# Routed rows kept on chip and filed whole into a slot-ordered DRAM buffer, in a cross-attention and mixture-of-experts layer

## The reference

```python
x = x + attention(layernorm(x), ctx)
X = layernorm(x).reshape(16384, 512)
scores = sigmoid(X @ gate_w.T)                      # 32 experts
_, idx = top_k(scores + bias, 4)
w = scores[idx] / sum(scores[idx])
pos = place of this choice among all choices of its expert, in token order
valid = pos < 512
xe[expert, pos] = X[token] where valid              # 32 x 512 x 512
ye = (silu(xe @ W1) * (xe @ W3)) @ W2               # inner width 256
out = sum over the 4 choices of w * ye[expert, pos] (0 where not valid)
out = out + (silu(X @ sw1.T) * (X @ sw3.T)) @ sw2.T
x = x + out
```

## Time and profile before

| | |
|---|---|
| time, median of 3 runs | 1765.65 us |
| lowest and highest | 1764.72 and 1767.5 us |
| the profiled execution's own time | 1765.1 us |
| its span in the trace | 1763.3 us |
| mean granted clock of TensorE, share of full speed | 0.975 |
| PE, DVE, POOL, ACT busy | 93%, 78%, 71%, 60% |
| moved by the DMAs | 293.75 MB, 167 GB/s |

### The profile page before, as it was taken

The page is one execution under the profiler, slowest core; times in us unless marked ns, Lnnn a source line. Parts: engine busy times, 40 slices in busy tenths (PEclk is TensorE's granted clock), DMA queues, the critical chain, the costliest instruction groups (busy, mean ns, idle before and its releaser), DMA issues. The chain is left out here.

```text
span 1763.3 us, 31937 instructions
## 1 busy us (share of the span) xinstructions
PE 1636.3 (93%) x9056; PEld 1020.9 (58%) x9056; DVE 1379.1 (78%) x3486; ACT 1066.7 (60%) x2368; POOL 1253.2 (71%) x1104
## 2 busy tenths in 40 slices
PE   5999999999999999999999999999758999999991
PEld 4566666666666666656666665655335555555550
DVE  5679988887998888889888888999636777677771
ACT  5676776767777677777767777775323444444440
POOL 2327777777777777777777777777776777887864
PEclk8999999999999999999999999999889999999995
DMA  7546776777776666678676667787439789998665
GB/s 255 150 128 162 196 167 165 172 169 158 166 187 174 156 174 165 158 174 189 161 155 174 164 161 181 178 202 164 125 121 280 154 179 166 203 214 153 100 91 74
DMA packets 474532, 293.75 MB, mean 167 GB/s; under 512 B 342643, under 2 KB 385397, under 8 KB 474356
## 3 DMA queue, kind: packets, MB, share of 16 engines
q1 hardware_dynamic: 429300, 239.03, 53.1%
q0 software_dynamic: 45056, 52.67, 18.4%
HBM read 135.06 MB, written 110.17 MB: 139 GB/s over the span
## 5 line engine op out<-in xcount | busy, mean ns | idle before, releaser
L923 POOL DMA_INDIRECT slot_table<-tok_line,slot x480 | 508.3, 1059 | 135.9 <-issue 126.3
L932 POOL TENSOR_TENSOR xt_l<-xt,xt_h 128x512 fp32r<-128x512 f32 x128 | 165.0, 1289 | 159.2 <-ACT xt_h L758 159.2
L799 ACT ACTIVATE prob<-S_ps,rs 128x512 f32<-128x512 f32 x128 | 88.1, 688 | 254.8 <-DVE S_ps L1295 248.3
L485 PE MATMUL S_ps<-a_h,xt_h 128*128 128x512 f32 x512 | 211.5, 413 | 3.4 <-DVE m_l L1268 3.3
L500 PE MATMUL O_ps<-m_h,pt_h 128*128 128x512 f16 x512 | 196.2, 383 | 14.5 <-DMA pt_l<-p_l 12.9
L485 PE MATMUL S_ps<-a_h,xt_l 128*128 128x512 f32 x512 | 200.9, 392 | 0.0
L485 PE MATMUL S_ps<-a_l,xt_h 128*128 128x512 f32 x512 | 200.8, 392 | 0.0
L500 PE MATMUL O_ps<-m_l,pt_h 128*128 128x512 f16 x512 | 194.7, 380 | 0.0
L500 PE MATMUL O_ps<-m_h,pt_l 128*128 128x512 f16 x512 | 194.7, 380 | 0.0
L947 POOL TENSOR_TENSOR prob<-prob,rsum 128x512 f32<-128x512 f32 x128 | 135.6, 1059 | 80.8 <-DVE rsum L1323 74.4
L1567 POOL DMA_INDIRECT out<-ye,idx_far x80 | 125.5, 1569 | 46.3 <-issue 22.7
(11 more groups left out here) (245 smaller groups left out, 4773.3 us busy)
## 6 DMA issues: line engine op xcount, KB each, us to landing
xt<-in_xT SPq DMA_DIRECT2D x128, 256.0 KB
xr<-in_x SPq DMA_DIRECT2D x64, 512.0 KB, 3.8
x2aug<-x SPq DMA_DIRECT2D x128, 256.0 KB
out<-xr SPq DMA_DIRECT2D x64, 512.0 KB, 3.4
up_more<-in_w SPq DMA_DIRECT2D x36, 256.0 KB, 5.0
slot_table<-tok_line,slot POOLq DMA_INDIRECT x512, 2.1
up_w<-in_w SPq DMA_DIRECT2D x28, 256.0 KB, 4.3
down_more<-in_w SPq DMA_DIRECT2D x18, 256.0 KB, 6.2
```

What stands on the lines that cost most here:

```text
L485: last = pe.matmul(S_ps[t % 2][:, :], left[:, kc, :], right[:, b % 2, kc, :], start=(m == 0), stop=(m == 3 * KD - 1))
L799: act.activation(prob[:, t % 2, :, :], S_ps[t % 2][:, :].rearrange("p (h j) -> p h j", h=H), ACT.Exp, scale=rs[:, q % 2, 0, t % 2:t % 2 + ...
L923: pool.indirect_dma_start(table, bass.IndirectOffsetOnAxis(ap=slot[:, g % 2, i, q:q + 1], axis=0), tok_line[:, g % 2, i, :], None, bounds_ ...
L932: pool.tensor_tensor(xt_l[:, t % 2, :, :], xt[:, t % 2, :, :], xt_h[:, t % 2, :, :].bitcast(F32), ALU.subtract).then_inc(xt_lo, 1)
```

## The change

The token's row, its 32 weights and its number are now put side by side in one on-chip row of 560 floats (2,240 bytes). A ring `kept` of nine such tiles takes the place of `x2`, `wfull` and `tok_line`; the last two tiles go into two buffers that are free by then (`aside`). POOL's indirect DMA writes the whole row into a DRAM buffer `slot_rows` at the token's slot. An expert's 512 rows thus lie one behind the other, and SP loads them with one plain DMA (`load_rows`). `x2aug`, `slot_table`, the stores of rows and weights, the loads of slot numbers and the 128 gathers are gone. A scatter-add takes its row numbers from the loaded rows.

Empty slots must hold zero rows, so `slot_rows` is blanked first: 32 stores of 128 x 2,240 floats (1.147 MB), two in each step `n` from 1 to 16 (`fill_slots`). ACT's `rows_scaled(t)` newly waits until tile t-9 has been filed, for tiles 5 to 8 until all blanks are stored. `TABLE` is 21 instead of 20, `wk` and `wv` share one buffer and are loaded anew for each pair of batches (`load_kv`, 14 loads of 768 KB). The ring of expert rows has 5 places instead of 6, that of `ye` 3 instead of 4, and SP loads the rows of expert e when expert e-5 has landed in `out`, with the weights of expert e+5 behind.

In an expert's step PE, ACT and DVE take the turns and the down products in alternation.

The diff, cut to its core:

```diff
-ROW = D + E
+LINE = 16
+ROW = D + E + LINE
+ROWS_KEPT, ASIDE = 9, B * S // P - 2
...
+                def fill_slots(e):
+                    if e == 0:
+                        sp.wait_ge(zero_set, 3)
+                    sp.dma_start(slots_of[e], blank).then_inc(fill_stored, 16)
...
-                    for r in range(TOKENS, TOKENS + PAD, P):
-                        sp.dma_start(x2aug[r:r + P, :], zrow).then_inc(fill_stored, 16)
-                        sp.dma_start(out[r:r + P, :], zrow[:, 0:D]).then_inc(fill_stored, 16)
-                    sp.wait_ge(zero_set, 3)
-                    sp.dma_start(table.rearrange("(e p c) l -> p e (c l)", e=E, p=P),
-                                 fill.rearrange("p (e c) -> p e c", e=E)).then_inc(fill_stored, 16)
+                        sp.dma_start(out[r:r + P, :], zrow).then_inc(pad_stored, 16)
...
+                    for e in range(2 * n - 2, 2 * n):
+                        if 0 <= e < E:
+                            fill_slots(e)
...
                 def rows_scaled(t):
-                    after(act, x2_lo, t - 1)
-                    after(act, x2_stored[t % 2], t // 2 * 16)
-                    act.activation(x2[:, t % 2, :], x_tile(t), ACT.Identity,
+                    if ROWS_KEPT - CHUNKS <= t < ROWS_KEPT:
+                        act.wait_ge(fill_stored, E * 16)
+                    if ROWS_KEPT <= t < ASIDE:
+                        act.wait_ge(*filed_until(t - ROWS_KEPT))
+                    act.activation(kept_row(t), x_tile(t), ACT.Identity,
...
                     for q in range(first, end):
                         pool.indirect_dma_start(
-                            table, bass.IndirectOffsetOnAxis(ap=slot[:, g % 2, i, q:q + 1], axis=0),
-                            tok_line[:, g % 2, i, :], None, bounds_check=SLOTS - 1, oob_is_err=False).then_inc(scattered[g % 2], 16)
+                            slot_rows, bass.IndirectOffsetOnAxis(ap=slot[:, g % 2, i, q:q + 1], axis=0),
+                            kept_tile(t), None, bounds_check=SLOTS - 1,
+                            oob_is_err=False).then_inc(rows_filed[t % ROWS_KEPT], 16)
...
+        def load_rows(e):
+            if e >= RING:
+                sp.wait_ge(added, (e - RING + 1) * 64)
+            sp.dma_start(rows[:, e % RING, :, :].bitcast(F32), rows_src[e]).then_inc(rows_loaded[e % RING], 16)
...
-        def gather(e):
...
-        file_last(0)
-        expert_steps(step)
+        for e in range(E):
+            scatter(e)
...
             if u is not None:
                 up(u, 0)
+            if t is not None:
+                turn(t, 0)
             if d is not None:
                 down(d, 0)
             if t is not None:
-                turn(t, 0)
+                turn(t, 1)
             if d is not None:
                 down(d, 1)
             if t is not None:
-                turn(t, 1)
                 turn(t, 2)
```

294 lines of the change are left out of this document (135 added, 159 removed).

## The result

The changed kernel takes 1836.76 us (median of 4 runs, 1834.36 to 1839.59), the kernel before 1766.58 us (4 runs beside it): **3.9% slower**, ratio 1.0393, 95% interval 1.0375 to 1.0412. The forecast was 1760, its range ended at 1790. The span of the profiled execution is 1832.5 us against 1763.3, 69.2 us longer.

The account below looks back on a forecast made before the run. PE was taken to bound the token stage, the chain of scatter-add landings the expert stage. Transition -28.9, expert stage -16.9, startup +38, token stage +3 gave -4.8 against 1765.1: 1760 us, range 1732 to 1790.

Parts of the forecast that it names:

- Startup: Start of the kernel: 32 blank stores, 91 us of all DMA engines, were to cost +38 us.
- +27 us: Startup: turned tile 1, behind twelve blanks on SP's queue, was to reach ACT at about 60 us instead of 32.8.
- +11: Startup, tile 1 to tile 11: the remaining 20 blanks were to add 11 us, from a span of +3 to +11.
- I take 8.7 to 9.5 us per tile for 8.4: Startup, tiles 1 to 11: assumed time per tile with blanks in the queue, giving +3 to +11 us.
- Transition: Between token and expert stages: without gathers and with list 0 filed early, first scatter-add at 1310, 28.9 us earlier.
- Order on PE: Expert stage: alternating turns and down products removes PE's 0.6 us wait per expert but was given no gain by itself.
- Token stage: Token tiles: whole-row filing, ACT's new filing wait and reloads of wk and wv were to cost +3 us (0 to 8).
- between nothing and 1 us, on an engine that is 60% busy: Token stage: size given to ACT's new wait, before scaling a row, for the filing of nine tiles before.
- Expert stage: Experts' loop: with scatters alone on POOL, 31 periods of 12.5 us plus 4 against 408.4 now, 16.9 us shorter.
- the chain is what the last rows show: 12.5 us: Expert stage: the scatter-add chain's period without gathers, read from the last rows, 12.5 us instead of 13.17.
- the chain gets no shorter: Rival, expert stage: row loads delay the next expert's scatters, period stays 13.17, 17 us not won, 1777 us; chance 0.2.
- some two steps later, 25 us against 6: no wait: Expert stage: expert e+5's rows, loaded once expert e has landed, were to arrive well before PE needs them.

Follow-up runs that it names:

- the gather run: The kernel before, with gathers also fetching the padding row for empty slots of experts 6 to 31: 1768.4 us, ratio 1.0005.
- the run without empty slots: The changed kernel, with scatter-adds that leave out empty slots and row loads as they are: 1779.8 us, ratio 1.0071.

## Why the prediction was wrong

**Startup: right mechanism, too small, and divided wrongly.** "+27 us" ahead of tile 1 came out as 26.7, "+11" behind it as 20.0. The step that failed is "I take 8.7 to 9.5 us per tile for 8.4": measured were (165.6 - 61.7) / 10 = 10.4. The run with tile 1 moved showed that the division means nothing: the DMA engines are full to 150 us, and whether tile 1 stands behind the first twelve blanks or ahead of them is worth 1 us at tile 11. The 28 further blanks, 80 us of DMA time at 402 GB/s, cost 42.6 us; the remaining half fitted beside the other loads. The forecast counted the DMA queue alone; that PE's own work to tile 11 takes 8.6 us longer at the lower granted clock was no term of it. How much of that would have hidden behind the DMAs was not separated. By the Trainium skill ("DMA: Bandwidth & Descriptors", section "Specifications"), about 358 GB/s, the forecast's term would have been an estimated 48 and not 38, and 46.7 were measured. That nearness is luck: the rate is not what this trace shows, which moved 377 GB/s in the window from 30 to 100 us.

**Transition: right.** -28.9 forecast, -27.9 measured. List 0 filed early, one load, and turns right behind the token work, as the timelines show: the load of expert 0's rows lands at 1366.5, PE's token work ends at 1367.6, and the filings end 24.0 us behind that (forecast: 23). No run takes the parts of this term one by one.

**Order on PE: right.** Nothing forecast, -0.4 us measured by itself.

**Token stage: the step that failed is "between nothing and 1 us, on an engine that is 60% busy".** The wait was named and dismissed. ACT's scaling of a row waits for the filing issued in the step before, and behind it on ACT stand the high halves that SP must see before it turns rows and then probabilities; PE waits for those. By itself such a wait was about as short as forecast, 24.2 us in 30 waits between 420 and 1290 us; what was missed is that it reaches PE. An engine's mean busy share says nothing about a wait in front of work that is due. At the tail, where POOL's filings come late and all together, two waits alone were 11.9 us. Instead of +3 it was 35.7. With a tenth tile, which takes ACT's wait to 0.6 us, 23.6 us less are lost up to the end of PE's token work, 16.3 of them behind tile 125; with the reloads moved as well 24.6 less from tile 11 on. The last 11.1 us stay open.

**Expert stage: the step that failed is "the chain is what the last rows show: 12.5 us".** In the last rows not only the gathers have ended but the loads of weights too: from 1700 us on, the trace of before shows hardly a packet but the scatter-adds' own, at a DMA share of 0.48 to 0.79. Under a row load and weights the landing took 7.5 us, and the period 13.77. The rival "the chain gets no shorter" had the place and the direction ("just when an expert's last scatter has landed, so under the next expert's scatters") but was priced at the old period, 13.17, and no lengthening, and got 0.2. The bound found by the runs: both transfers wait for one event, so the DMA engines stand empty for about 2 us per expert and then have more than the period holds. Moving the load gave 22 us back, fewer scatter packets 57 with this input; the mere bytes in the old place cost nothing (the gather run). A second step was wrong, "some two steps later, 25 us against 6: no wait". PE's waits in the whole execution:

```profile
PE TE_ps L1609 <- DMA rows<-slot_rows: 24.1, 18, 3.6
```

PE ran ahead of the slower chain until the ring of five was full; from expert 12 on the load released by the chain comes just when PE needs it. This wait follows the chain and does not set it: an expert's first scatter-add is issued some 50 us after its first turn, and some 30 us after it in the run without empty slots, where PE never waits for rows. With the row load in four pieces the period rose to 14.34; why is open. The Trainium skill ("DMA: Bandwidth & Descriptors", "Queues, rings and completion order") states that an engine drains a whole packet of one queue before it turns to the next; I had taken from it that smaller pieces would let the scatter-adds through sooner, and that run does not bear this out.

The sum with measured terms is 26.7 + 20.0 + 21.3 + 14.4 - 27.9 + 14.7 = 69.2 us.

## What to carry to other kernels

When a transfer becomes contiguous and leaves an engine, look at the bytes that it now always moves (blanks, empty slots) and at the event that starts it: two transfers that wait for the same event can leave the DMA engines empty before it and crowded after, as here. A wait on an engine that is far from busy is priced by what stands behind it, down to the bound engine. A chain's length read from the last rows of a loop holds only for the traffic of those rows.

## What the runs showed of the hardware that was not expected

An indirect DMA costs POOL the same for a row of 2,240 bytes as for a line of 64 (1061 ns both over the whole span). That holds where the rows really move: the first eight tiles carry more than half of all filed bytes, and their 32 filings, first with the change, then before, are

```profile
L952 POOL DMA_INDIRECT slot_rows<-kept,slot x32 | 33.7, 1052 | 8.6 <-issue 8.6
L923 POOL DMA_INDIRECT slot_table<-tok_line,slot x32 | 34.1, 1064 | 8.6 <-issue 8.5
```

Blanks on POOL's own DMA queue, begun 13 to 14 us earlier, delayed the turned probabilities by up to 22.7 us and tile 11 by 77 us, where the same bytes on SP's queue, in program order with the loads, delayed tile 11 by 47. A scatter-add whose rows are partly or all out of bounds (58% of them here) frees the DMA engines but not POOL: its four issues per expert still stand 1.86 us apart.
